# Attention and routed feed-forward on one core: float32 scalars for the one-hot comparisons, and eight weight halves moved between the block table's operations

## What is computed

```python
x = x + xattn(layernorm(x), ctx, ctx, Wq, bq, Wk, bk, Wv, bv)      # 16 x 256 x 256, ctx 16 x 120 x 256
h = layernorm(x).reshape(-1, 256)                                   # 4096 rows
topk_vals, topk_idx = top_k(h @ Wr.T + br, 2)                       # 8 experts
topk_w = softmax(topk_vals)
for e in range(8):
    cw = sum(topk_w * (topk_idx == e), axis=-1)
    out += cw[:, None] * (gelu(h @ W1[e].T + b1[e]) @ W2[e].T + b2[e])   # W1[e]: 1024 x 256
z = out + h
x = x + (layernorm(z) * ln_w + ln_b)
```

## Time and profile before

| | |
|---|---|
| median of 3 runs | 671.07 us (666.03 to 672.51) |
| the profiled execution | 672.68 us, of which 671.0 us are the span on the core |
| TensorE busy | 575.4 us, 86% |
| DVE busy | 451.5 us, 67% |
| POOL busy | 322.8 us, 48% |
| ACT busy | 285.7 us, 43% |

### The profile page before, as it was taken

One profiled execution on the slowest core, in us unless ns is written; L12 is line 12 of the kernel. 1 busy time (PEld: TensorE's weight loads), 2 busy tenths in 40 slices (PEclk: granted clock), 3 DMA queues, 4 the chain that ended last, 5 costly groups with the idle time before them and its releaser, 6 DMA issues.

```text
span 671.0 us, 18378 instructions
## 1 busy us (share of the span) xinstructions
PE 575.4 (86%) x5001; PEld 511.9 (76%) x5002; DVE 451.5 (67%) x1373; ACT 285.7 (43%) x700; POOL 322.8 (48%) x501
## 2 busy tenths in 40 slices
PE   6999989999737999999999999999999999995000
PEld 5899889888625898989989898989898998674000
DVE  1589998889873675757575766667575756553585
ACT  2687767666324424243333333342424333331342
POOL 3024432434314265665555464556465554633596
PEclk9999999889657999999999999999999999999555
DMA  6356665455423032323323232323232322321843
GB/s 213 104 178 195 183 205 150 154 180 186 131 65 127 18 58 44 60 40 56 41 54 47 48 47 48 47 48 55 41 61 41 55 35 41 49 33 19 239 142 125
DMA packets 56916, 61.49 MB, mean 92 GB/s; under 512 B 9480, under 2 KB 52432, under 8 KB 56752
## 3 DMA queue, kind: packets, MB, share of 16 engines
q1 hardware_dynamic: 38896, 37.94, 18.4%
q0 software_dynamic: 13632, 18.91, 18.0%
q10 hardware_dynamic: 4352, 4.20, 1.8%
HBM read 39.00 MB, written 22.02 MB: 91 GB/s over the span
## 4 chain that ended last, share of the span: by engine, by line
PE 70%; DVE 12%; POOL 6%; issue 5%; DMA 2%; ACT 2%; DVEq 1%; SPq 0%; POOLq 0%; ACTq 0%
PE bank L820 10%; PE bank L822 9%; PE bank L821 9%; PE bank L842 9%; PE bank L843 9%; PE bank L844 9%; PE bank L685 2%; PE bank L799 2%; POOL w1hi L624 2%; PE bank L730 2%; DVE st L1074 2%; PE bank L776 1%; PE bank L705 1%; DMA sums_dram<-xn,mt 1%; POOL w1lo L617 1%
## 5 line engine op out<-in xcount | busy, mean ns | idle before, releaser
L980 ACT ACTIVATE stage<-bank,mt 128x256 f32<-128x256 f32 (+1 forms) x312 | 125.0, 452 | 179.2 <-PE bank L822 148.4
L580 POOL DMA_INDIRECT sums_dram<-xn,mt x71 | 114.3, 1609 | 132.6 <-DVE xn L1240 117.0
L820 PE MATMUL bank<-xnt,w1hi 128*128 128x256 f16 (+1 forms) x624 | 164.4, 265 | 7.4 <-DVE xnt L1213 3.7
L821 PE MATMUL bank<-xnt,w1hi 128*128 128x256 f16 (+1 forms) x624 | 163.8, 264 | 0.0
L822 PE MATMUL bank<-xnt,w1lo 128*128 128x256 f16 (+1 forms) x624 | 163.7, 264 | 0.0
L842 PE MATMUL bank<-w2hi,stage 128*128 x568 | 154.9, 273 | 2.4 <-DVE xn L1240 2.2
L843 PE MATMUL bank<-w2lo,stage 128*128 x568 | 154.8, 273 | 0.0
L844 PE MATMUL bank<-w2hi,stage 128*128 x568 | 154.8, 273 | 0.0
L1222 DVE CAST stage<-stage 128x512 f16<-128x512 f32 (+1 forms) x156 | 74.5, 478 | 114.3 <-PE bank L844 113.5
L1224 DVE TENSOR_TENSOR stage<-stage 128x512 f16<-128x512 f32 (+1 forms) x156 | 102.3, 655 | 5.4
L564 POOL DMA_INDIRECT xg<-tokens_dram,mt x71 | 74.4, 1047 | 50.1 <-PE bank L799 30.8
(11 more groups left out here) (184 smaller groups left out, 956.5 us busy)
## 6 DMA issues: line engine op xcount, KB each, us to landing
stage<-in_L_ffn_W_dram SPq DMA_DIRECT2D x16, 768.0 KB, 5.1
x<-in_x_dram SPq DMA_DIRECT2D x16, 256.0 KB, 4.7
tokens_dram<-xn SPq DMA_DIRECT2D x16, 256.0 KB, 2.2
sums_dram<-xn SPq DMA_DIRECT2D x16, 256.0 KB, 2.8
stage<-in_L_ffn_W_dram SPq DMA_DIRECT2D x16, 256.0 KB, 3.8
w1hi<-sums_dram SPq DMA_DIRECT2D x16, 256.0 KB, 4.3
out_dram<-w1hi ACTq DMA_DIRECT2D x16, 256.0 KB, 2.4
ctx_sb<-in_ctx_dram SPq DMA_DIRECT2D x16, 120.0 KB, 4.1
```

The lines of the kernel that those rows point to most:

```text
L580: nc.gpsimd.indirect_dma_start(out=sums_dram, out_offset=bass.IndirectOffsetOnAxis(ap=sidx[p][:, t:t + 1], axis=0), in_=y_sb[p][:, t, :], ...
L820: nc.tensor.matmul(dst, w1hi[:, col], xhi[:, k, 0:bt], start=(k == 0), stop=False)
L821: nc.tensor.matmul(dst, w1hi[:, col], xlo[:, k, 0:bt], start=False, stop=False)
L980: ins = nc.scalar.activation(h32[:, c * bt:(c + 1) * bt], f_h[q][:, (c % 2) * bt:(c % 2 + 1) * bt], ACT.Gelu, bias=b1s[p][:, c:c + 1], sca ...
```

## The change

The two index tiles become one tile `seat_at` of int32, a new `tensor_copy` casts its eight columns to float32 (`seat_f`), and the comparisons take their scalars from there. `codes` becomes a float32 tile. A semaphore count (`SLOTTED`) grows from 5 to 6, since the comparisons now wait for the cast. In the block table, seven of the last eight low halves are put between the operations, one behind the wait for `rank_kept` and six behind others; the eighth stays behind the last operation.

```diff
-        codes = sb("codes", [P, NT], I32)
+        codes = sb("codes", [P, NT])
-        seat_row = sb("seat_row", [P, TJ * TOPK], I32)
-        seat_unit = sb("seat_unit", [P, TJ * TOPK], I32)
+        seat_at = sb("seat_at", [P, 2, TJ * TOPK], I32)
+        seat_f = sb("seat_f", [P, 2, TJ * TOPK])
-        SLOTTED = 5
+        SLOTTED = 6
@@ publish, on DVE
+                if publish is not None:
+                    dve.wait_ge(slot_self, SLOTTED * k + 5)
+                    nc.vector.tensor_copy(seat_f[:, :, :], seat_at[:, :, :]).then_inc(slot_self, 1)
                 if publish is not None:
                     at_least(dve, seats_mm, k)
-                    dve.wait_ge(slot_self, SLOTTED * k + 5)
+                    dve.wait_ge(slot_self, SLOTTED * k + 6)
                     for i in range(TJ * TOPK):
-                        nc.vector.tensor_scalar(hot_row[i], seat_iota[:, 0:P], seat_row[:, i:i + 1], None, ALU.is_equal)
-                        ins = nc.vector.tensor_scalar(hot_unit[i], seat_iota[:, :], seat_unit[:, i:i + 1],
+                        nc.vector.tensor_scalar(hot_row[i], seat_iota[:, 0:P], seat_f[:, 0, i:i + 1], None, ALU.is_equal)
+                        ins = nc.vector.tensor_scalar(hot_unit[i], seat_iota[:, :], seat_f[:, 1, i:i + 1],
                                                       codes[:, bass.ds(TJ * k + i // TOPK, 1)], ALU.is_equal, ALU.mult)
@@ the block table, on DVE
             dve.wait_ge(rank_kept, NB)
+            late_groups(low_part, 0, 1)
             chain(nc.vector.tensor_scalar(cnt, b_rank[:, 0, :], float(P - 1), None, ALU.add))
...
             chain(nc.vector.tensor_scalar(all_odd, all_odd, float(E), None, ALU.is_equal))
+            late_groups(low_part, 1, 2)
...
             chain(nc.vector.tensor_scalar(ends, ends, float(TB * FULL), None, ALU.min))
+            late_groups(low_part, 2, 3)
...
             nc.vector.tensor_copy(seat_token, token_f).then_inc(seats_ready, 1)
+            late_groups(low_part, 6, 7)
             dve.wait_ge(spare_ready, 1)
...
-            late_groups(low_part, 0, 8)
+            late_groups(low_part, 7, 8)
```

More of the change, by code:

```diff
@@ L498, in _ @@
             nc.gpsimd.iota(seat_iota[:, :], [[1, SEATS]], base=0, channel_multiplier=0, allow_small_or_imprecise_dtypes=True)
-            nc.gpsimd.iota(codes[:, 0:NB], [[P, NB]], base=-TOK // 2, channel_multiplier=1)
-            nc.gpsimd.iota(codes[:, NB:], [[P, NB]], base=1, channel_multiplier=1).then_inc(consts_pool, 1)
+            nc.gpsimd.iota(codes[:, 0:NB], [[P, NB]], base=-TOK // 2, channel_multiplier=1, allow_small_or_imprecise_dtypes=True)
+            nc.gpsimd.iota(codes[:, NB:], [[P, NB]], base=1, channel_multiplier=1,
+                           allow_small_or_imprecise_dtypes=True).then_inc(consts_pool, 1)
             tick = [1]
@@ L1097, in step @@
                     dve.wait_ge(slot_self, SLOTTED * k + 4)
-                    nc.vector.tensor_scalar(seat_row[:, :], slots[:, :], P - 1, None, ALU.bitwise_and)
-                    nc.vector.tensor_scalar(seat_unit[:, :], slots[:, :], P.bit_length() - 1, None, ALU.arith_shift_right).then_inc(slot_self, 1)
+                    nc.vector.tensor_scalar(seat_at[:, 0, :], slots[:, :], P - 1, None, ALU.bitwise_and)
+                    nc.vector.tensor_scalar(seat_at[:, 1, :], slots[:, :], P.bit_length() - 1, None, ALU.arith_shift_right).then_inc(slot_self, 1)
                 if project is not None:
@@ L1175, in _ @@
             chain(nc.vector.tensor_tensor_scan(rest_ends, ones[:, 0:E], rest, 0.0, ALU.mult, ALU.add))
+            late_groups(low_part, 3, 4)
             parts_of = ((slice(0, FULL), FULL, ends, taken), (slice(FULL, BLOCKS), SHORT, rest_ends, hops))
@@ L1191, in _ @@
             chain(nc.vector.tensor_scalar(rowf[:, FULL:], rowf[:, FULL:], taken[:, 0:1], None, ALU.add))
+            late_groups(low_part, 4, 5)
             nc.vector.tensor_scalar(beyond, jota[:, 0:FULL], ends[:, E - 1:E], float(SEATS), ALU.is_ge, ALU.mult)
@@ L1198, in _ @@
             chain(nc.vector.tensor_copy(code_f, b_seats))
+            late_groups(low_part, 5, 6)
             nc.vector.memset(token_f[:, SEATS:], float(TOK // 2 - 1))
```

## The result

| | before | changed |
|---|---|---|
| median | 670.42 us (666.03 to 673.53, 17 executions) | 675.04 us (673.09 to 680.37, 17 executions) |
| profiled execution, its span | 672.68 us, 671.0 us | 673.09 us, 671.4 us |
| first product of the blocks | 208.41 us | 208.95 us |

The changed kernel takes 1.0079 times as long, with an interval of 1.0058 to 1.0101: 3.9 to 6.8 us more, or 4.6 us between the medians. This is inside the border of 1%, and it is not zero.

A forecast was written before the change was run, and what follows sets the result against it. The prediction took the gathers behind the block table to set the first block product's start: 4.6 us for moved halves and 0.4 for the clock made 5.0, casts 1.2, comparisons 0, so +6.2 us to 677.3; range 670 to 683.

The forecast's parts named there:

- What bounds the kernel: Ahead of the first block product, L820: the gathers set its start, closely behind the weights; delaying the table delays them.
- gather path: From the table's signal seats_ready through GpSimd's index copy and gather to L820; behind the weight path by 0.1 to 0.8 us.
- weight path: The last low half ends at 207.41 and L820 starts 1.0 us later; with the change, weights done 3.5 us earlier, unused.
- The moved halves: In the block table: seven halves ahead of seats_ready add 4.2 us, plus waits of 0.24 and 0.45; signal 4.9 us later.
- the path behind the signal: From seats_ready to L820: GpSimd follows at its distances; the half no longer ahead of x_low gives back some 0.2 us.
- The clock term: At the first block products: TensorE starts at the lower clock after standing some 6 us; 0.4 us taken, 0 to 0.9 possible.
- The comparisons: L1111 and L1112 in the one-hot steps: float32 scalars in place of int32 save 0 us.
- The casts: Sixteen casts in the attention steps: 0.20 us each in six uncovered places, 1.2 us; hidden in the loop; bounds 0 and 3.2.
- Rival (a): Attention steps: comparisons get shorter, saving 4.2 us, and GpSimd's norm loses its stretch, 1.3; total 670.6 us; chance 0.12.
- (b): Attention steps: the cast waits for GpSimd's operation, 4.2 us in the loop and 2.5 elsewhere; total 684 us; chance 0.08.
- (c): First block product: low halves, not gathers, set its start; -3.5 us, +1.2 for casts, total 668.8 us; chance 0.05.
- (d): Attention part: the places where TensorE's clock falls shift by some us; total 668 to 682 us; chance 0.13.

The follow-up runs named there:

- the second edit alone: Kernel before with only the seven low halves moved between the block table's operations, int32 scalars kept; 674.35 us, ratio 1.0087.
- three halves moved: Kernel before with three low halves instead of seven moved into the block table, int32 scalars kept; 674.46 us, ratio 1.0073.
- the two kernels without a slow product: Seven halves moved, int32 scalars, plus 24 useless products ahead of the first gather's landing (672.11 us); kernel before plus twelve useless products at the start (666.79 us).
- the 24 useless products: Seven halves moved, int32 scalars, plus 24 useless float32 products on TensorE between the seats' signal and the first gather's landing; 672.11 us, ratio 1.0045 against the kernel before.
- the first edit alone: Kernel before with only the cast and the float32 scalars, the eight low halves left behind the table; 671.36 us, ratio 1.0018.
- the kernel of the thin halves: Kernel before with the last eight low halves 8 columns wide instead of 512, the rest zeros written early by GpSimd; one execution, 673.05 us.
- twelve useless products: Twelve useless float32 products on TensorE at the start: in the kernel before 666.79 us, ratio 0.9969; in the changed kernel, one wait later, 679.21 us, ratio 1.0168.
- with twenty: Kernel before with early gathers and twelve useless products at the start, plus sixteen in the table wait and four before the first gathered block; 665.05 us, ratio 0.9947.

## Why the prediction came out as it did

The forecast was 677.3 us, 6.2 more than before. Measured were 4.6 by the medians and 5.3 by the ratio, with the mechanism named in the prediction.

**What bounds the kernel.** Right. The gather path was put 0.1 to 0.8 us behind the weight path. With the weight path taken away it was 0.45, in one execution.

**The moved halves.** Right, in each term. Forecast was a signal 4.9 us later: it was 4.7 in the changed kernel, 4.8 in the second edit alone. The first moved half was to wait 0.24 us and the third, behind ScalarE's table load, 0.45; they waited 0.23 and 0.36. The first product was to come 4.6 us later. It was 4.3, since the path behind the signal lost 0.4 to 0.5 us where the prediction gave back 0.3. The wait of 8.27 us ahead of L800 is longer than the forecast 6, because the transposes ran earlier; the mechanism is the same.

**The clock term.** The first product came at the lower clock, as forecast (0.39 us), but the cost was not what was taken: 0.4 us, with 0 to 0.9 as bounds, all for the fast part ahead of the slow stretch of before. In the profiled pair the term is -0.3. What failed was the step that took the slow stretch of before as given. The distance from the first product to the next transposes is 6.91 us before, 6.59 changed, 6.96 with the second edit alone, 8.18 with three halves moved, and 5.24 and 5.25 in the two kernels without a slow product. So up to 3 us hang on it, and before already paid 1.7 of them. Over many executions the only measure is the 2.8 us that the 24 useless products brought back, with intervals that overlap. In the profiles they take 1.7 us out of this place and cost 1.1 ahead of it. Another 2.5 us are gone at two later places, where the second edit alone was slow and the kernel before wasn't, so they don't belong to this term.

**The comparisons.** Right: 0 us, by L1240 against L1200. The same operation now stands in both forms, 247 with an int32 scalar and 254 with a float32 one, and 339 and 341. The Trainium skill, DVE: scalar operands, raw-bit mode, write accounting and state across instructions, section Scalar operands, says that an int32 index needs no cast ahead of it, and the trace now agrees: the cast bought nothing.

**The casts.** Right in kind, too large in size: +1.2 us forecast, +0.7 in the profile of the first edit alone (0.5 in the steps, 0.2 behind them). The six uncovered places at 0.20 are near what was found: against the kernel before, the first three steps grow by 0.01, 0.08 and 0.18 us, the last four by 0.29 less 0.09, 0.17 and 0.21, and the piece behind them by 0.2, together 1.05. What failed is the loop, which was put at nothing and gave 0.3 us back. Its four steps at a granted clock of 1.00 became 0.07 to 0.08 shorter each, its three at 0.84 stayed as they were. The cover is there, as it was said: the half behind the comparisons waits no more for ScalarE. And GpSimd's norm, which took 0.36 us beside the comparisons in all eight steps of the loop, took 0.20 in seven of them and 0.26 in one. The rows of the changed kernel that answer to the earlier trace rows and to the second of the earlier trace rows:

```profile
114.70 0.20 POOL L518 TENSOR_TENSOR rn<-nmu,rn 128x4 f32<-128x4 f32 x1
...
116.16 0.68 DVE L1046 SCALAR_TENSOR_TENSOR w2lo<-bank,w2hi 128x512 f32 x1
```

Rival (a) had this stretch of 0.16 us gone together with shorter comparisons. It went, and the comparisons are not shorter. Whether the later start of the comparisons or the kind of their scalar did it, no run tells apart.

**The rivals.** (a), shorter comparisons, fell with their durations. (b), a cast held by GpSimd, fell too. The sixteen casts take 156 to 181 ns, and twelve of them, at 156 to 168, start inside GpSimd's operation of 0.7 to 1.1 us. The rule of the Trainium skill behind it, SBUF — State Buffer, section SBUF: two separate sides, would, as the prediction read it, have held them to the end of that operation. These casts don't show it; the rows at the end of this document, beside an iota and a memset, do. (c) fell with the time itself, and with the kernel of the thin halves, where the first product did not follow the weights. (d) is real. The profiled pair differs by -4.6 us in such places, and they made this pair look equal.

That the change cost 1 to 2 us less than the forecast has three sources in the profiles: the casts (0.5 too much), the path at the table (0.3 too much) and the clock term (0.7 too much, in this pair of executions). They are of the size of the differences between groups of runs.

## What to carry to other kernels

Before filling an engine's wait with another engine's work, follow both inputs of the next operation. Here two paths were 0.45 us apart, so the fill could win 0.45 us at the most, and it put 4.7 us on the other path. Put late work behind the signal that somebody waits for, or make the waiting work wait for less. Cast an operand only if a row shows that its type costs something. And don't read a difference of a few us from one pair of profiles: add it up by stretches and set aside those that the change can't reach. Compare steps only where the granted clock is the same, and when the same addition goes into a second kernel, see that it starts at the same time there.

## What the runs showed of the hardware

The places where the granted clock falls to the lower level are worth more here than either edit. The same kernel's executions before spread over 7 us, and twelve useless products moved the time by -2.1 us in the kernel before and, starting 1.2 us later, by some +6 us in the changed one. With 24 useless products just ahead of the first product of the blocks its slow stretch went away; with twenty, of which the last four ended 0.9 us ahead of the gathered block, it did not. What decides between these isn't settled.

The clock's record does not show every such place. It says 1.00 for the kernel before from 8 to 12 us, where the eight bias products take 1.86 us that take 1.05 in the changed kernel. It says 1.00 from 16 to 20 us as well, where the eight products of L730 take 2.67 us, as long as those of L734 in the changed kernel with twelve products, for which it says 0.50.

A small operation of DVE between SBUF tiles is stretched beside a GpSimd iota or memset. The comparison beside the iota took 0.39 us. The same one, with no iota beside it in the changed kernel, takes 0.23:

```profile
194.25 0.23 DVE L1199 TENSOR_SCALAR work<-work 128x7 f32<-128x7 f32 x1
```

In the kernel with the thin halves the iota fell on another operation, and that one took 0.39 instead of 0.18:

```profile
195.06 0.39 DVE L1189 CAST eid<-work 128x39 int32<-128x39 f32 x1
...
195.06 0.36 POOL L552 IOTA work<- 128x272 f32 x1
```

The zeros of that kernel show it more strongly. GpSimd's memset ends at 191.07, and an operation of 8 columns that takes 0.17 us in the kernel before (L1160) lasts until 191.10:

```profile
187.61 3.46 POOL L545 MEMSET w2lo<- 128x4032 f16 x1 [0.16 <-POOL gate_oh L539]
...
190.30 0.80 DVE L1163 TENSOR_SCALAR work<-work 128x8 int32<-128x8 int32 x1
```

Its 0.63 us more, less the 0.16 that the iota no longer costs at its old place, are the 0.5 us by which the table took longer in that kernel (9.62 against 9.13). Neither the comparisons nor the casts show such a hold beside GpSimd's longer operation on four columns. That one reads SBUF tiles and computes, while iota and memset only write; whether this is what tells the cases apart was not tried.
